# Mixture-of-experts stage with the up product turned round, the two halves of the tokens on one contraction, and one load per page

## The reference, cut to what matters

```python
top_probs, top_idx = jax.lax.top_k(softmax(x @ gate_w + gate_b), 2)
h1 = einsum('bsd,edh->bseh', x, w1); h2 = einsum('bsd,edh->bseh', x, w2)   # d 64, e 16, h 128
hidden = silu(h1) * h2
expert_out = einsum('bseh,eho->bseo', hidden, w3)
y = einsum('bseo,bse->bso', expert_out, dispatch)        # dispatch: the two weights of a token
```

## Time and profile before

| | us |
|---|---|
| median of 3 runs (lowest, highest) | 543.08 (538.88, 543.24) |
| span of the profiled execution | 598.9 |
| PE busy in it (matmuls 4186) | 500.9 (84%) |
| PEld busy | 436.7 (73%) |
| DVE busy | 441.6 (74%) |
| ACT busy | 396.0 (66%) |
| POOL busy | 287.9 (48%) |

### The profile page before, as it was taken

The page is one execution under the profiler, slowest core; times in us unless marked ns, Lnnn a source line. Parts: engine busy times, 40 slices in busy tenths (PEclk is TensorE's granted clock), DMA queues, the critical chain, the costliest instruction groups (busy, mean ns, idle before and its releaser), DMA issues.

```text
span 598.9 us, 14226 instructions
## 1 busy us (share of the span) xinstructions
PE 500.9 (84%) x4186; PEld 436.7 (73%) x4186; DVE 441.6 (74%) x1242; ACT 396.0 (66%) x946; POOL 287.9 (48%) x378
## 2 busy tenths in 40 slices
PE   6899997896986627767889899999999999999854
PEld 5566665674764516757878799999998999899753
DVE  4567786685689697556676688888888888888653
ACT  5577885684765303456676588888787878778650
POOL 4000036666667675645555455454444544545351
PEclk9878997996979557879999899999999999999986
DMA  7941101011000012320122221232242425210404
GB/s 295 283 84 36 35 12 61 25 60 62 25 24 29 22 46 66 69 63 21 39 56 57 54 43 39 51 90 54 48 116 49 118 55 147 55 31 17 134 24 141
DMA packets 62664, 40.97 MB, mean 68 GB/s; under 512 B 50003, under 2 KB 54318, under 8 KB 62080
## 3 DMA queue, kind: packets, MB, share of 16 engines
q1 hardware_dynamic: 52208, 23.84, 17.5%
q0 software_dynamic: 8800, 8.94, 4.4%
q10 hardware_dynamic: 1584, 7.29, 3.2%
HBM read 21.46 MB, written 19.19 MB: 68 GB/s over the span
## 4 chain that ended last, share of the span: by engine, by line
PE 51%; DVE 17%; ACT 10%; issue 9%; another core or an unknown queue 6%; DMA 4%; SPq 3%; POOLq 0%; DVEq 0%; ACTq 0%; POOL 0%
PE up L971 9%; PE up L973 8%; PE turn L987 6%; PE up L803 5%; PE lines L1004 5%; PE small L819 3%; ACT xc L703 3%; DVE hidden L1589 2%; DMA x_in<-in_x 2%; PE lines L1006 2%; PE small L848 2%; PE up L789 2%; PE small L952 2%; PE up L778 2%
## 5 line engine op out<-in xcount | busy, mean ns | idle before, releaser
L519 POOL DMA_INDIRECT results<-result,page_in x147 | 154.3, 1050 | 152.0 <-ACT xc L703 103.5
L498 POOL DMA_INDIRECT pages<-payload,slot_int x128 | 127.6, 997 | 141.7 <-DVE slot_int L1414 73.5
L971 PE MATMUL up<-up_w,xs_hi 128*128 x588 | 163.5, 310 | 9.8 <-issue 5.1
L973 PE MATMUL up<-up_w,xs_lo 128*128 x588 | 150.0, 287 | 0.3 <-issue 0.3
L703 ACT ACTIVATE xc<-up 128x512 f32<-128x512 f32 x147 | 89.5, 609 | 76.5 <-PE up L973 48.4
L971 PEld LDWEIGHTS up<-up_w,xs_hi 128*128 128x128 f32 x588 | 114.1, 194 | 16.2 <-issue 13.7
L973 PEld LDWEIGHTS up<-up_w,xs_lo 128*128 128x128 f32 x588 | 114.7, 195 | 0.0
L1589 DVE SCALAR_TENSOR_TENSOR hidden<-up,page_in,xc 128x128 f32<-128x128 f32 x196 | 59.4, 344 | 43.2 <-ACT xc L703 35.4
L1599 DVE TENSOR_TENSOR hidden_lo<-turn,hidden_hi 128x512 f16<-128x512 f32 x98 | 67.0, 684 | 3.9 <-ACT hidden_hi L716 2.8
L987 PE MATMUL turn<-ident,hidden 128*128 128x128 f32 x392 | 60.7, 279 | 2.8 <-DVE branch L1599 1.6
L716 ACT ACTIVATE hidden_hi<-turn 128x512 f16<-128x512 f32 x98 | 60.9, 622 | 3.1 <-PE turn L987 2.5
(11 more groups left out here) (262 smaller groups left out, 999.2 us busy)
## 6 DMA issues: line engine op xcount, KB each, us to landing
pages<-up_w ACTq DMA_DIRECT2D x4, 1332.0 KB, 9.9
page_in<-pages SPq DMA_DIRECT2D x147, 36.0 KB
page_in<-pages SPq DMA_DIRECT2D x147, 32.0 KB
x_in<-in_x SPq DMA_DIRECT2D x7, 512.0 KB
out<-up_raw SPq DMA_DIRECT2D x5, 512.0 KB, 4.8
results<-result,page_in POOLq DMA_INDIRECT x147
up_raw<-in_L_ffn_w SPq DMA_DIRECT2D x4, 512.0 KB, 16.8
pages<-payload,slot_int POOLq DMA_INDIRECT x128
```

The costliest lines, as they stand in the source:

```text
L498: pool.indirect_dma_start(out=pages, out_offset=bass.IndirectOffsetOnAxis(ap=slot_int[q % PAYLOADS][:, t:t + 1], axis=0), in_=payload[q % ...
L519: pool.indirect_dma_start(out=results, out_offset=bass.IndirectOffsetOnAxis(ap=page_in[g % LOADS][:, k, D + AT_TOKEN:D + AT_TOKEN + 1].bit ...
L971: pe.matmul(target, xs_hi[g % 2][:, k * P:(k + 1) * P], weights[:, bass.ds(e * 2, 2 * HID)], start=True, stop=False)
L973: last = pe.matmul(target, xs_lo[g % 2][:, k * P:(k + 1) * P], weights[:, bass.ds(e * 2, 2 * HID)], start=False, stop=True)
```

## The change

One version of the page stage is put in the place of another. In words, engine by engine:

- **SP** loads each page once (72 floats a token).
- `turn_rows` transposes 64 columns a page into 64 partitions. ACT writes the high half (16 bit, scaled by 2^12) into partitions 0 to 63 of a tile `xs`, DVE the low half into partitions 64 to 127. One contraction over 128 partitions then takes both halves.
- `up_product`: the expert's weights are the stationary tile and the tokens move. `up_w` holds, per expert, four 128x128 tiles of 16 bit: gates high, gates low, values high, values low. So a page takes 16 matmuls of 128 columns, first the eight of the gates (semaphore `gates_ready`), then the eight of the values (`up_ready`), each with a stationary tile of its own and an address of its own. The result has the hidden axis on the partitions.
- `turn_hidden` is gone. ACT's two scalings (L707) are gone. `hide` is one instruction of 128x512.
- `down_product`, three pages behind: on even pages (`split`) three matmuls of 64 columns per expert on 16-bit halves (which ACT and DVE make from `hidden` on these pages alone), on odd pages one float32 matmul per expert on `hidden` and `down_raw`. Each expert has PSUM columns of its own.
- The weights of the tokens come behind the down product: DVE `weigh`, once per two pages, multiplies 2x4x64 columns. POOL adds the four experts in two steps per group (`sum_up`, 512 and 256 columns), in order between its scatters; DVE does so for the last 11 pages (`tail_sum`).
- Ten turns back go through the bank `lines` and no longer through `turn`. The low and high halves of `up_w` are made later in the first part, both with scales; `blank`, the zeros written into `pages`, lies in `x2`.

```diff
-    STRIDE = 2 * D
+    STRIDE = D
...
-    LAG = 4
+    LAG = 3
+    RING = 4
...
-        up_w = sb("up_w", [P, E, 2, HID], F32R)
+        up_w = sb("up_w", [P, E, 2, 2, HID], F16)
...
-                    sp.dma_start(page_in[g % LOADS][:, k, D:D + ROW], at).then_inc(page_loaded[g % LOADS], 16)
-                    sp.dma_start(page_in[g % LOADS][:, k, 0:D], at[:, 0:D]).then_inc(page_loaded[g % LOADS], 16)
+                    sp.dma_start(page_in[g % LOADS][:, k, :], pages[bass.ds(row, P), :])\
+                        .then_inc(page_loaded[g % LOADS], 16)
...
+            def sum_up(g):
+                pool.wait_ge(weighed_done, 2 * g + 2)
...
+                pool.tensor_tensor(halves[:, :, :, :], parts[:, :, 0:2, :], parts[:, :, 2:4, :], ALU.add)\
+                    .then_inc(halved, 1)
...
+                pool.tensor_tensor(result[g % LOADS][:, :, :], halves[:, :, 0, :], halves[:, :, 1, :], ALU.add)\
+                    .then_inc(summed, 1)
...
             def silu(n):
-                act.wait_ge(up_ready, n + 1)
+                act.wait_ge(gates_ready, n + 1)
...
-                for j in range(SCALED):
-                    last = act.activation(scaled[n % 2][:, j * HID:(j + 1) * HID],
...
             def up_product(n, experts):
...
+                weights = up_w[:, :, :, :, :].rearrange("p e m a h -> p (e m a h)")
+                at = slice(k * P, (k + 1) * P)
+                for m in range(2):
+                    for j, e in enumerate(experts):
+                        target = up[n % 2][:, m * CW + j * P:m * CW + (j + 1) * P]
+                        high = weights[:, bass.ds(e * (4 * HID // STRIDE) + 2 * m * HID, HID)]
+                        low = weights[:, bass.ds(e * (4 * HID // STRIDE) + (2 * m + 1) * HID, HID)]
+                        pe.matmul(target, high, xs[g % 2][:, at], start=True, stop=False)
+                        last = pe.matmul(target, low, xs[g % 2][:, at], start=False, stop=True)
+                    last.then_inc((gates_ready, up_ready)[m], 1)
...
+            def down_product(n, experts):
...
+                    if split(n):
+                        own_hi = high_low[:, bass.ds(e * 2, D)]
+                        pe.matmul(target, hidden_hi[n // 2 % 2][:, at], own_hi, start=True, stop=False)
+                        pe.matmul(target, hidden_lo[n // 2 % 2][:, at], own_hi, start=False, stop=False)
+                        last = pe.matmul(target, hidden_hi[n // 2 % 2][:, at], high_low[:, bass.ds(e * 2 + D, D)],
+                                         start=False, stop=True)
+                    else:
+                        last = pe.matmul(target, hidden[n % RING][:, at], whole[:, bass.ds(e, D)], start=True, stop=True)
                 last.then_inc(down_done, 1)
...
-                if 0 <= n - 2 < PAGES:
-                    turn_hidden(n - 2)
...
             def hide(n):
...
+                dve.scalar_tensor_tensor(out=hidden[n % RING], in0=up[n % 2][:, CW:HW], scalar=hidden_scale[:, 0:1],
+                                         in1=act_s[n % 2], op0=ALU.mult, op1=ALU.mult).then_inc(hidden_done, 1)
...
+            def weigh(m):
+                g, k = 2 * m // BY, 2 * m % BY
+                count = min(2, PAGES - 2 * m)
+                dve.wait_ge(down_done, 2 * m + count)
+                if k == 0 and g >= 2:
+                    if g - 2 < SUMMED:
+                        dve.wait_ge(halved, g - 1)
...
```

More of the change, by code:

```diff
@@ L501, in scatter, with sums_behind @@
                         .then_inc(scattered[q % PAYLOADS], 16)
+            sums = 0
+            def sum_up(g):
+                pool.wait_ge(weighed_done, 2 * g + 2)
+                if g:
+                    pool.wait_ge(summed, g)
+                parts = weighed[g % 2]
+                pool.tensor_tensor(halves[:, :, :, :], parts[:, :, 0:2, :], parts[:, :, 2:4, :], ALU.add)\
+                    .then_inc(halved, 1)
+                pool.wait_ge(halved, g + 1)
+                if g >= LOADS:
+                    pool.wait_ge(returned[g % LOADS], 16 * BY * (g // LOADS))
+                pool.tensor_tensor(result[g % LOADS][:, :, :], halves[:, :, 0, :], halves[:, :, 1, :], ALU.add)\
+                    .then_inc(summed, 1)
+            def sums_behind(silus):
+                nonlocal sums
+                while sums < SUMMED and BY * sums + 8 <= silus:
+                    sum_up(sums)
+                    sums += 1
             for q in range(PAIRS):
@@ L741, in _ @@
+            rows_high(0)
+            for n in range(PAGES + 1):
                 if n < PAGES:
                     silu(n)
-                if n % BY == 2 and n // BY + 1 < GROUPS:
+                if n % BY == 0 and n // BY + 1 < GROUPS:
                     rows_high(n // BY + 1)
+                if n >= 1 and split(n - 1):
+                    hidden_high(n - 1)
             for q in range(EARLY, PAIRS):
@@ L1581, in hide @@
             def hide(n):
-                g, k = n // BY, n % BY
-                if n >= 3:
-                    dve.wait_ge(hidden_turned, n - 2)
-                values = up[n % 2][:, :].rearrange("p (j m h) -> p j m h", j=PER_LINE, m=2)[:, :, 1, :]
+                if n >= RING:
+                    dve.wait_ge(down_done, n - RING + 1)
+                dve.wait_ge(up_ready, n + 1)
                 dve.wait_ge(silu_done, n + 1)
-                for j in range(SCALED, PER_LINE):
-                    at = slice(j * HID, (j + 1) * HID)
-                    dve.scalar_tensor_tensor(
-                        out=hidden[n % 3][:, at], in0=values[:, j, :],
-                        scalar=page_in[g % LOADS][:, k, D + AT_WEIGHT + j:D + AT_WEIGHT + j + 1],
-                        in1=act_s[n % 2][:, at], op0=ALU.mult, op1=ALU.mult)
@@ new lines, in tail_sum @@
+            def tail_sum(m):
+                g, k = 2 * m // BY, 2 * m % BY
+                count = min(2, PAGES - 2 * m)
+                dve.wait_ge(weighed_done, m + 1)
+                if m == 2 * SUMMED:
+                    dve.wait_ge(summed, SUMMED)
+                else:
+                    dve.wait_ge(result_ready, m - 2 * SUMMED)
+                parts = weighed[g % 2][:, k:k + count, :, :]
+                dve.tensor_tensor(halves[:, 0:count, :, :], parts[:, :, 0:2, :], parts[:, :, 2:4, :], ALU.add)\
+                    .then_inc(tail_halved, 1)
+                dve.wait_ge(tail_halved, m - 2 * SUMMED + 1)
@@ L1624, in add_input @@
                                          in1=x2[:, q, cols(c)], op0=ALU.mult, op1=ALU.add).then_inc(back_read, 1)
[L1626 to L1632 removed]
+            for n in range(PAGES + LAG + 2):
                 if n < PAGES:
                     hide(n)
+                if 0 <= n - 1 < PAGES and split(n - 1):
+                    hidden_low(n - 1)
+                if n >= LAG + 1 and (n - LAG - 1) % 2 == 0 and n - LAG - 1 < PAGES:
+                    m = (n - LAG - 1) // 2
+                    weigh(m)
+                    if 2 * m >= LAST:
+                        tail_sum(m)
                 if 2 <= n < 10:
```

258 lines of the change are left out of this document (100 added, 158 removed).

## The result

The changed kernel takes 731.96 us (median of 4 runs, 725.34 to 734.89) against 543.16 (4 runs, 538.88 to 544.23): a ratio of 1.348, 95% interval 1.342 to 1.353. It is slower, as forecast, but by 189 us and not by 37. The profiled execution took 725.34 us, 723.0 of them span.

A forecast was written before the change was run, and what follows sets the result against it. PE's sequencer was to bound the changed page stage: issue of 9.42 us per four pages, 2.36 a page against 2.065, gave +37 us with +5 for stalls and +1 for the first part: 580 us, own range 555 to 610, overall 503 to 620.

The forecast's parts named there:

- the price of an address: PE's sequencer: a stationary tile's address costs 0.032 to 0.046 us, middle 0.039, beside 0.0405 us to issue a pair.
- up product: PE's issue of 16 addresses and pairs a page: 1.27 us, 5.09 us per four pages; array 0.88 us a page.
- expert numbers: PE's sequencer loads four expert numbers a page, unchanged, at 0.338 us each: 1.35 us per four pages.
- even down: Issue of the split down product on even pages: 0.80 us each, 1.60 us per four pages.
- odd down: Issue of the float32 down product on odd pages: 0.48 us each, 0.96 us per four pages.
- waits and transposes: PE's sequencer per four pages: waits 0.26 us, at 0.051 us each, and four transposes 0.16 us.
- signs of being right: Page stage: some 20 address operations a page, up matmuls 0.07 to 0.09 us apart, silu to silu 2.2 to 2.5 us.
- the bounds 1.10 to 2.55: POOL's new sums of 512 and 256 columns: 1.10 to 2.55 us, taken as 1.8, hidden under PE.
- The stalls of the first stretch: Before the change, 231 to 350 us: 32 us of PE stalls, taken mostly for the profiler's own.
- Rival A: Page stage: issue doesn't bind; POOL, array and DVE lie close at some 1.8 us a page, 505 us; chance 0.27.
- Rival B: PE's array: weight loads don't hide, 0.075 us a matmul, 1.9 us a page, about 540 us; chance 0.10.
- Rival C: PE's granted clock falls too, three tenths of the time at 1.2 GHz, 2.61 us a page: 623 us; chance 0.11.

## Why the prediction was wrong

Its mechanism was right: the sequencer's issue sets the page, and "each of the 16 has a stationary tile of its own, thus an address of its own". The step that failed is the price of an address, put at 0.032 to 0.046 us, with the 0.0405 us to issue a pair beside it. What the earlier trace rows gave was only a sum, 0.113 us for one address and two pairs. I took the address from its record in the earlier trace rows and put what was left on the pairs. It is the other way round: two pairs per address cost what one does (732.84 against 731.96 us), and the address has nearly the whole 0.124. The row was at hand: the lone sum of the earlier trace rows, taken as the price of an address whatever stands behind it, would have given 16 x 0.113 = 1.81 us for the up product instead of 1.27. The trace of the kernel before had even more: from one start to the next, 350 to 545 us, its FUSED_REGOPS takes a median of 0.124 us, its ALU_OP 0.113 and its load 0.399, against records of 0.046, 0.032 and 0.338. With these, 22 addresses and a load come to 22 x 0.124 + 0.399 = 3.13 us a page, where the forecast had 2.36 for everything and 3.39 was measured.

The Trainium skill says in "Perfetto Trace Analysis", section "Sequencer-only Instruction (DRAIN, etc)", how little such a record holds: the profile shows only the instruction's execution; fetching and decoding ahead of it and the push behind it are in no record. This trace agrees, with 0.124 us from start to start at a record of 0.046; what fills the rest, no run here shows.

Point by point, per four pages, forecast and measured (counts times the means of the table): up product 5.09 and 64 x 0.131 = 8.4 us; expert numbers 1.35 and 4 x 0.397 = 1.6; even down 1.60 and 16 x 0.131 = 2.1; odd down 0.96 and 8 x 0.123 = 1.0; waits and transposes 0.42 and 94 / 22 x 0.118 = 0.5. Together 9.42 and 13.6 us, 3.4 a page. Four fifths of the miss are the up product's addresses. The other terms that grew have the same reason: the loads and the waits, too, were priced by their records (0.338 and 0.051), not by what follows them. Two of the prediction's signs of being right therefore failed: the up matmuls start 0.124 us apart and not 0.07 to 0.09, and a page takes 3.39 us and not 2.2 to 2.5.

The rest held. The array idles under the issue; ACT is busy for a third; DVE waits for PE, and POOL for a silu that waits for PE; the load that went is worth nothing. POOL's two steps that add up the four experts cost 1.26 + 0.76 = 2.0 us a group by their records, within the bounds 1.10 to 2.55, and are hidden. The estimate by the Trainium skill ("GPSIMD Engine Reference", section "Performance versus the Vector engine"), 2.2 us, was near. The stalls of the first stretch were that profiled execution's own, as taken: the run with one load a page doesn't have them, nor does the run with an address more per step, which has both loads (first silu at 211.7 us, not 231.8).

**Rival A** (issue doesn't bind) fell: its 505 us were for addresses that cost little, and a free one leads to 534. **Rival B** fell: 16 more weight loads a page cost nothing, and with a full queue a pair takes 0.056 us, not the 0.075 of the rival. The rule of the Trainium skill that stood behind it ("TensorE: Matmul & The Clock Gate", section "Back-to-back issue gap", 81 ns a pair) is not what this chip did here. **Rival C** was right that the clock falls (0.82 to 0.86), and wrong that it costs: at 1.00, with every up matmul doubled, the time is the same.

The range reached to 2.51 us a page for an address at the end of its bracket. That bracket was made of two records of the operation itself and had no row in it that held what the operation delays, as the earlier trace rows does.

## What to carry to other kernels

Price a sequencer's instruction by the usual distance from its start to the next start, not by its record, and count the addresses that come from registers, not matmuls. To see whether a sequencer is the limit, look for long distances among these, not at their sum. Where the operand is chosen at run time, lay the data out so that one address serves two or more matmuls: here the split of high and low belongs over the partitions of the operand that is chosen, not of the one that isn't. A kernel can become bound by issue through a change that takes work from the array: here the up product went from 8 x 0.120 to 16 x 0.056 us, four transposes a page went, and the kernel became slower by a third.

## What the runs showed of the hardware

- On PE's sequencer an address (FUSED_REGOPS) took a median of 0.124 us start to start with one 16-bit pair behind it or two, 0.120 with float32 pairs, at granted clocks from 0.71 to 1.00 alike; an ALU_OP of the kernel before took 0.113. On average an up matmul's was 0.131: some distances were 0.15 to 0.28 us. Why, no run here shows.
- A load of four values into registers took 0.397 us until the next start, one of eight 0.65; a wait on a semaphore that held nothing up 0.106 to 0.126.
- The granted clock, from 300 to 400 us: a mean of 0.71 with 712 matmuls, 0.83 in the changed kernel with 800, 1.00 with 1207 or 1260, but 1.00 also with the 804 of the run in which every down product is float32. So the number of matmuls alone doesn't set it; what does, no run here shows. It did not make the pace: 732.84 us at 1.00, 731.96 in the changed kernel.
